# Plain attention: queries and keys projected with heads in partitions, moved to the pairs' rows by DMA; the maxima of four heads turned together

## The reference

```python
x = L0_attn_x                                  # (8, 512, 256) float32
xn = layernorm(x)
x = x + attn_rotary(xn, ...) + ffn(xn, ...)    # both read xn
# ffn(src): 16 heads of 16, this is the part at hand
q = src @ Wq + bq; k = src @ Wk + bk; v = src @ Wv + bv
scores = einsum('bqhd,bkhd->bhqk', q, k) * 16 ** -0.5
attn = softmax(scores) @ v @ Wo + bo
x = layer_norm(src + attn, ln1_g, ln1_b)
# then each row goes through one of 4 experts (256 -> 1024 -> 256), and a second layer_norm
```

## Time and profile before

| | |
|---|---|
| median of 3 runs | 2095.5 us (2095.2 to 2095.9) |
| profiled execution | 2098.55 us, its span 2096.8 us |
| TensorE busy | 1861.5 us (89%) |
| VectorE, ScalarE, GpSimd busy | 1308.8, 915.6, 985.6 us |
| score exponentials of the first phase | 256 x 1025 ns, 248.3 us |
| maxima reductions of the first phase | 512 x 682 ns, 323.2 us |
| maxima products of the first phase | 512, 161.3 us |

### The profile page before, as it was taken

How to read it: one execution, slowest core, us unless ns; L and a number is a source line. 1 busy time by engine, 2 the same in 40 slices (tenths; PEclk the granted TensorE clock), 3 DMA queues, 4 the chain that set the end, 5 groups by cost and what they waited for, 6 DMA issues and landing times.

```text
span 2096.8 us, 36970 instructions
## 1 busy us (share of the span) xinstructions
PE 1861.5 (89%) x12145; PEld 1131.9 (54%) x12146; DVE 1308.8 (62%) x2894; ACT 915.6 (44%) x1313; POOL 985.6 (47%) x681
## 2 busy tenths in 40 slices
PE   5999999999998109999479999999999999999998
PEld 3454544544543109999455555646556565554654
DVE  3767677677675416777676565765656666565661
ACT  2657566566566004444225244252432515335152
POOL 2414133242344353544337637385473855738454
PEclk8999999999999659999779999999999999999999
DMA  6300000000002244566400010100101001010000
GB/s 176 131 1 11 10 0 10 10 0 10 0 0 101 91 176 183 213 213 234 114 11 2 11 32 1 42 2 11 32 1 42 2 11 32 1 42 1 15 18 11
DMA packets 56176, 104.86 MB, mean 50 GB/s; under 512 B 7238, under 2 KB 46566, under 8 KB 50156
## 3 DMA queue, kind: packets, MB, share of 16 engines
q1 hardware_dynamic: 52972, 94.71, 13.4%
q0 software_dynamic: 3072, 8.39, 1.2%
HBM read 76.35 MB, written 26.74 MB: 49 GB/s over the span
## 4 chain that ended last, share of the span: by engine, by line
PE 38%; issue 6%; DVE 3%; POOL 2%; ACT 1%; POOLq 0%; DMA 0%; DVEq 0%; ACTq 0%; SPq 0%
PE a_psS L703 10%; PE a_psO L717 10%; PE a_psO L740 6%; PE a_psM L677 5%; PE a_psS L665 4%; PE a_psS L649 2%; PE a_psS L730 1%; POOL a_k_tok L350 1%; ACT a_probs L468 1%; DVE a_junk L534 1%; POOL a_oT L373 1%; POOL a_q_tok L350 1%; DVE a_alibi L611 0%; DVE a_qL L524 0%; DVE a_rden L548 0%
## 5 line engine op out<-in xcount | busy, mean ns | idle before, releaser
L385 POOL TENSOR_TENSOR a_probs<-a_probs 128x1024 f32<-128x1024 f32 x144 | 340.8, 2393 | 315.9 <-PE a_psO L717 315.9
L534 DVE CUSTOM_DVE_ANT_0 a_junk<-a_psM,a_alibi 128x512 bf16<-128x512 f32 x512 | 333.7, 689 | 215.0 <-PE a_psM L677 214.1
L1282 DVE TENSOR_REDUCE f_q_tok<-f_psR 128x1 f32<-128x512 f32 x512 | 323.2, 682 | 136.6 <-PE f_psR L1437 136.0
L468 ACT ACTIVATE a_probs<-a_psS 128x1024 f32<-128x1024 f32 x256 | 248.8, 1024 | 284.0 <-PE a_psS L703 283.9
L1220 ACT ACTIVATE f_probs<-f_psS 128x1024 f32<-128x1024 f32 x256 | 248.3, 1025 | 64.0 <-PE f_psS L1456 63.4
L717 PE MATMUL a_psO<-a_probs,a_v 128*32 128x512 f32 x2048 | 244.0, 597 | 0.0
L1437 PE MATMUL f_psR<-f_kP,f_qM 64*128 64x512 f32 x512 | 161.3, 498 | 25.6 <-DVE f_q_tok L1282 17.9
L677 PE MATMUL a_psM<-a_kH,a_qH 64*128 64x512 f32 x512 | 126.3, 488 | 34.0 <-DVE a_n_tok L534 29.0
L1469 PE MATMUL f_psO<-f_probs,f_v 128*32 128x512 f32 x1024 | 136.4, 604 | 0.7 <-ACT f_probs L1220 0.6
L740 PE MATMUL a_psO<-a_wo,a_oT 128*128 128x256 f32 x512 | 131.2, 404 | 4.4 <-POOL a_oT L373 4.4
L1843 ACT ACTIVATE e_h<-e_psH,w_o 128x256 f32<-128x256 f32 x152 | 63.8, 471 | 148.7 <-PE e_psH L1935 148.7
(11 more groups left out here) (201 smaller groups left out, 3783.3 us busy)
## 6 DMA issues: line engine op xcount, KB each, us to landing
w_w_high<-w_parts SPq DMA_DIRECT2D x19, 1024.0 KB, 5.5
w_w_low<-w_parts SPq DMA_DIRECT2D x19, 1024.0 KB, 7.6
sorted_x<-f_zeros SPq DMA_DIRECT2D x1, 4864.0 KB, 21.2
e_xs<-sorted_x SPq DMA_DIRECT2D x19, 256.0 KB, 2.7
sorted_z<-e_z SPq DMA_DIRECT2D x19, 256.0 KB, 2.2
f_xn<-in_L_attn_x SPq DMA_DIRECT2D x8, 512.0 KB, 3.5
f_w_raw<-in_L_ffn_W SPq DMA_DIRECT2D x4, 1024.0 KB, 9.2
w_parts<-f_w_high SPq DMA_DIRECT2D x4, 1024.0 KB, 3.9
```

The costliest lines, as they stand in the source:

```text
L385: nc.gpsimd.tensor_tensor(slots, slots, probs[:, first - GRP:first - GRP + 2, :], ALU.add).then_inc(added.sem, 1)
L468: nc.scalar.activation(probs[:, slots, :], psS[:, 2 * p:2 * p + 2, :], ACT.Exp).then_inc(exp_done.sem, 1)
L534: nc.vector.tensor_tensor_reduce(out=junk[:, a, :], in0=psM[:, a, :], in1=alibi[:, h, :], scale=1.0, scalar=-3.0e38, op0=ALU.add, op1=ALU.max,
L1282: nc.vector.tensor_reduce(q_tok[:, c, h, NEG:NEG + 1], psR[:, ring_bank("max", u), :], AX.X, ALU.max, negate=True).then_inc(max_done.sem, 1)
```

## The change

Projection: `project` now has the weights as the stationary operand and the rows of x as the moving one, so that a psR bank holds 128 columns of q or k (64 of each half) by 512 rows of x. The four sides of a batch are keys and queries of the pairs 0 to 3, and keys and queries of the pairs 4 to 7. The weights' columns are put in that order by eight scalings ahead of batch 0. ScalarE takes each side twice out of its bank, whole and high, with the bias (`take_sides`), GpSimd subtracts (`low_part`), and twelve DMAs from SBUF to SBUF for each half of the pairs put the rows where the products want them (`move_sides`): kP and qP, one copy for both kinds of product. The maxima go to a small tile n_tok; when a quad's are complete, four small transposes turn them, ScalarE copies them (4 partitions, n_row), and two DMAs write them to the two rows in qP (`move_maxima`). The 24 groups of transposes of keys and queries are gone. A half is moved when the last scores that read the old one are through (r7 and r15; r is 4 quad + j), and the first maxima product that reads it waits for all twelve (in r10 and, for the second half, in r2 of the next batch). AHEAD is 24 products instead of 20. The projections of queries and keys stand in r4 to r7 instead of r6 to r9, and all maxima products are spread evenly, four a period. On SP the write of zeros, the preloads and the first w1 load come behind the moves of batch 0; stores and loads of w1 for experts 0 and 1 behind those of batch 1. On GpSimd the splits have moved too. VectorE's loop over batches is written out.

```diff
-    AHEAD = MQ + 2
+    AHEAD = 2 * (MQ + 4)
...
     EXTRAS = {(0, 1): [("v", 1)], (0, 2): [("out", 0), ("out", 1)], (0, 3): [("out", 2), ("out", 3)],
-              (1, 2): [("proj", 0)], (1, 3): [("proj", 1)], (2, 0): [("proj", 2)], (2, 1): [("proj", 3)],
+              (1, 0): [("proj", 0)], (1, 1): [("proj", 1)], (1, 2): [("proj", 2)], (1, 3): [("proj", 3)],
               (3, 3): [("v", 0)]}
...
+    TURNED = {(0, 2): [("maxima", 1, 0)], (0, 3): [("rows", 0, 0), ("rows", 1, 2)], (1, 2): [("maxima", 2, 0)],
+              (2, 2): [("maxima", 3, 0)], (3, 2): [("maxima", 0, 0)]}
...
-        quad, j = divmod(r, TT)
-        if quad == QUADS - 1:
-            products = [[0, 1], [2, 3, 4], [5, 6, 7], [8, 9]][j]
-        else:
-            products = [m for m in (AHEAD + 2 * r, AHEAD + 2 * r + 1) if m < QUADS * MQ]
-        return [[2 * m + a for m in part for a in range(2)] for part in (products[:1], products[1:])]
+        first = (AHEAD + 4 * r) % (2 * QUADS * MQ)
+        return [first, first + 1], [first + 2, first + 3]
...
+            def move_sides(b, g):
+
+                if not (isinstance(b, int) and b == 0):
+                    sp.wait_ge(score_ps.sem, score_ps.at(b - 1, QP * (2 * g + 2) * TT - 1))
+                    sp.sem_inc(passed, 1)
+                for i, (pair_rows, kinds) in enumerate(((kP, (high, low, high)), (qP, (high, high, low)))):
+                    n = 2 * g + i
+                    sp.wait_ge(low_done.sem, low_done.at(b, n))
+                    sp.sem_inc(passed, 1)
+                    for a in range(2):
+                        for k, part in enumerate(kinds):
+                            first = FB * a + FH * k
+                            sp.dma_start(pair_rows[first:first + FH, HP * g:HP * (g + 1), :].bitcast(F32),
+                                         part[FB * a:FB * (a + 1), n, :].bitcast(F32)).then_inc(moved[g].sem, 16)
+
+            def move_maxima(b, quad):
+
+                sp.wait_ge(n_row_done.sem, n_row_done.at(b, quad))
+                for a in range(2):
+                    row = FB * a + NEG
+                    sp.dma_start(qP[row:row + 1, QP * quad:QP * (quad + 1), :].bitcast(F32),
+                                 n_row[QP * a:QP * (a + 1), quad % 2, :].bitcast(F32)).then_inc(n_moved.sem, 16)
...
+            sp.wait_ge(zeroed, ZEROED)
+            heads = w["Wo"].rearrange("(q i d) n -> i d q n", i=4, d=FH)
+            for i in range(4):
+                sp.dma_start(wo[32 * i:32 * i + FH, :, :], heads[i]).then_inc(wo_in, 16)
+            move_sides(0, 0)
+            load_rows(0)
+            move_maxima(0, 0)
+            move_sides(0, 1)
+            sp.dma_start(sorted_x.rearrange("(n p) d -> p n d", p=P),
+                         zeros[:, :].unsqueeze(1).to_broadcast([P, TILES * TOK // P, D])).then_inc(cleared, 16)
+            for tile, source in preloads:
+                sp.dma_start(tile, source).then_inc(preloaded, 16)
+
+            def batch(b, more, last):
+                move_maxima(b, 1)
+                move_maxima(b, 2)
+                if more:
+                    if not last:
+                        load_rows(b + 1)
+                    move_sides(b + 1, 0)
+                move_maxima(b, 3)
+                if more:
+                    move_maxima(b + 1, 0)
+                    move_sides(b + 1, 1)
+
             load_w1(0)
-            load_rows(0)
-            for e in range(EARLY):
+            batch(0, True, False)
+            for e in range(NE // 2):
                 store_w1(e)
                 load_w1(e + 1)
-            with sp.Fori(1, B - 1) as b:
-                load_rows(b)
-            for e in range(EARLY, NE):
+            with sp.Fori(1, B - 2) as b:
+                batch(b, True, False)
+            batch(B - 2, True, True)
+            batch(B - 1, False, True)
+            for e in range(NE // 2, NE):
                 store_w1(e)
                 if e + 1 < NE:
                     load_w1(e + 1)
...
+            def low_part(b, n, first=False):
+
+                if not first:
+                    pool.wait_ge(moved[n // 2].sem, moved[n // 2].at(b - 1, 1))
+                    pool.sem_inc(passed, 1)
+                pool.wait_ge(high_done.sem, high_done.at(b, n))
+                pool.sem_inc(passed, 1)
+                nc.gpsimd.tensor_tensor(low[:, n, :], whole[:, n % 2, :], high[:, n, :],
+                                        ALU.subtract).then_inc(low_done.sem, 1)
...
                     norm0.raise_variance(pool, b + 1)
                 if before:
                     normalize(b - 1, QUADS - 1)
-                for e in splits[0:1]:
-                    split_w1(e)
                 add_bias_to_rows(b, not before)
                 if more:
                     keep_rows(b + 1)
+                    low_part(b + 1, 0)
                 normalize(b, 0)
-                for e in splits[1:]:
+                if more:
+                    low_part(b + 1, 1)
+                for e in splits[0:1]:
                     split_w1(e)
-                if more:
...
                 normalize(b, 1)
                 if more:
-                    reset_last(b + 1)
-                    low_last(b + 1)
+                    low_part(b + 1, 2)
+                    low_part(b + 1, 3)
                 if before:
                     scale_rows(b - 1)
                 normalize(b, 2)
                 if before:
                     finish_rows(b - 1)
-
-            batch(0, False, True, range(EARLY))
+                for e in splits[1:]:
+                    split_w1(e)
+
+            batch(0, False, True, range(NE // 2))
             with pool.Fori(1, B - 1) as b:
                 batch(b, True, True)
-            batch(B - 1, True, False, range(EARLY, NE))
...
+            for c in range(KC):
+                for i in range(2):
+                    for g in range(2):
+                        columns = raw[:, c, i, 2 * FB * g:2 * FB * (g + 1)].rearrange("p (e a d) -> p a d e", e=HP, a=2)
+                        nc.scalar.mul(wqk[:, c, 2 * g + i, :].rearrange("p (a d e) -> p a d e", a=2, d=FH), columns,
+                                      FH ** -0.5 if i else 1.0).then_inc(scaled, 1)
...
+            def take_sides(b, n, first=False):
+
+                bank = psR[:, ring_bank("proj", n), :]
+                if not first:
+                    act.wait_ge(moved[n // 2].sem, moved[n // 2].at(b - 1, 1))
+                if not first or n > 1:
+                    act.wait_ge(low_done.sem, low_done.at(b, n - 2))
+                act.wait_ge(proj_ps.sem, proj_ps.at(b, n))
+                nc.scalar.activation(whole[:, n % 2, :], bank, ACT.Identity, bias=bqk[:, n:n + 1])
+                nc.scalar.activation(high[:, n, :], bank, ACT.Identity, bias=bqk[:, n:n + 1]).then_inc(high_done.sem, 1)
...
+                if not first:
+                    act.wait_ge(n_moved.sem, n_moved.at(batch, n - 2))
+                act.wait_ge(nT_ps.sem, nT_ps.at(batch, n))
+                nc.scalar.copy(n_row[:, n % 2, :], psS[0:4, bank, :]).then_inc(n_row_done.sem, 1)
...
+                column = 4 * (pair // 2) + 2 * a + pair % 2
...
-                nc.vector.tensor_reduce(q_tok[:, c, h, NEG:NEG + 1], psR[:, ring_bank("max", u), :], AX.X, ALU.max,
+                nc.vector.tensor_reduce(n_tok[:, c, column:column + 1], psR[:, ring_bank("max", u), :], AX.X, ALU.max,
                                         negate=True).then_inc(max_done.sem, 1)
...
-                        last = nc.tensor.matmul(bank, xnT[:, c, n * P:(n + 1) * P], wqk[:, c, :],
+                        last = nc.tensor.matmul(bank, wqk[:, c, n, :], xnT[:, c, :],
                                                 start=(c == 0), stop=(c == KC - 1))
-                last.then_inc(proj_ps.sem, 1)
+                    last.then_inc(proj_ps.sem, 1)
...
+                else:
+                    pe.wait_ge(max_done.sem, max_done.at(batch, 2 * MQ * (n + 1) - 1))
+                    for t in range(TT):
+                        last = nc.tensor.transpose(psS[0:4, bank, t * P:(t + 1) * P], n_tok[:, t, 4 * n:4 * n + 4],
+                                                   idn[:, :])
+                    last.then_inc(nT_ps.sem, 1)
...
-                batch, half = b + belongs("max", u), HALVES[a]
-                if c == 0 and a == 0:
-                    pe.wait_ge(kP_done.sem, kP_done.at(batch, pair))
-                    pe.wait_ge(qM_done.sem, qM_done.at(batch, pair))
+                batch, half = b + belongs("max", u), slice(FB * a, FB * a + NEG)
+                if c == 0 and a == 0 and pair % HP == 0:
+                    pe.wait_ge(moved[pair // HP].sem, moved[pair // HP].at(batch, 1))
                 bank_read(b, "max", u)
-                nc.tensor.matmul(psR[:, ring_bank("max", u), :], qM[half, pair % 2, c * P:(c + 1) * P],
+                nc.tensor.matmul(psR[:, ring_bank("max", u), :], qP[half, pair, c * P:(c + 1) * P],
```

(47 more changed lines are left out.)

274 lines of the change are left out of this document (77 added, 197 removed).

## The result

The changed kernel takes 2156.7 us (2153.3 to 2162.8, four runs) against 2095.4 us for the kernel before, run beside it: a ratio of 1.0298, 95% interval 1.0269 to 1.0327. Its profiled execution took 2159.9 us, span 2158.1. All of it lies in the first phase: the next one begins (first DMA of w_idn) at 767.00 us instead of 706.39, 60.6 us later.

What follows compares the result with a forecast made beforehand. TensorE was taken to bound the kernel before, waits for the moves afterwards. Six batches +52, start +32, batch 1 +15 and last batch +3 gave +102 us on the median 2095.5: 2197 us, range 2047 to 2220.

Steps and rivals of the forecast that it cites:

- the likeliest one: Main forecast for the whole kernel: moves hold up TensorE twice a batch, 2197 us, own range 2165 to 2220, chance 0.55.
- halves once more from 32 partitions to 16: Assumed rate of the moves' DMAs onto 16 partitions: a quarter of 387 GB/s, 97 GB/s.
- M: Time of one move, twelve DMAs for half the pairs: 16.2 us of transfer plus 2.2 fixed, 18.4 us.
- The batch without stands: Steady batch of the first phase without waits for moves: four pieces together 70.0 us, against 80.4 before.
- The clock loss: After each TensorE stand for a move, four busy microseconds at about half clock: 2 us lost, twice a batch.
- the formula: Steady batch time: 48.2 us plus the larger of 9.2 and M plus the larger of 12.6 and M; 85.0.
- Start +32: One-off cost in batch 0, from late first moves and quad 1's maxima queued behind the zero fill: +32 us.
- Batch 1 and the last: One-off costs: batch 1's output waiting behind the W1 queue and split, +15 us; last batch, split 3 about 3 late, +3.
- Rival 1: Moves are hidden at the 32-partition rate or more: M 10.5 us, 2052 us; chance 0.32 together with Rival 3.
- Rival 2: Moves run halfway, at 135 GB/s: M 13.9 us, 2110 us; chance 0.13.
- Rival 3: VectorE becomes the bound even with short moves: 75 us a batch, 2075 us; chance 0.32 together with Rival 1.
- The signs: Expected in the profile: moves at about 100 GB/s, maxima waits of 5 to 9 us, quad 1 scores waiting some 12 us.

Runs made afterwards that it cites:

- e3: Changed kernel with only one DMA of each six in the moves, most pair rows keeping old values, timing only: 2057.9 us, ratio 0.9825.
- e5: Changed kernel with W1's first store and second load ahead of batch 0's second-half moves, last split after the last normalize: 2139.4 us, ratio 1.0212.
- e10: e8 with quad 0's move put ahead of quad 2's maxima rows and the load of x in SP's queue: 2044.5 us, ratio 0.9766.
- e9: Changed kernel with the two loops that order a half's twelve DMAs exchanged, same DMAs: 2152.2 us, ratio 1.0268.
- e1: Changed kernel with twelve DMAs of half the bytes each (256 of 512 tokens), timing only: 2091.5 us, ratio 0.9973.
- e2: Changed kernel with six whole DMAs of a half's twelve, so half the bytes, timing only: 2081.6 us, ratio 0.9936.
- e7: e4 plus e5's edits, with zero fill, preloads and first W1 load behind quad 1's maxima rows: 2074.3 us, ratio 0.9898.
- e8: e7 with VectorE's inversion of a quad's sums behind the round's second pair of maxima instead of ahead: 2063.5 us, ratio 0.9831.
- e4: Changed kernel projecting and moving by quads, each quad once scored, 48 half-size DMAs a batch for 24: 2108.3 us, ratio 1.0049.

## Why the prediction was right in sign and too high in size

**The mechanism held.** Slower was forecast, and the range 2047 to 2220 holds 2156.7; the likeliest one's own range (2165 to 2220) misses it by 8 us. TensorE waits twice a batch for the last of twelve DMAs with everything queued behind, the granted clock falls to 0.50 after the longer of the two waits and at times after the other, batch 0 waits for the rows of quad 1, batch 1's output for a split of W1, as described. e3, e5 and e10 each take their part away again.

**The move was mis-sized: 18.4 us, measured 14.9 by itself and 11.9 to 14.9 behind a load of x.** The step that failed is the rate: that it "halves once more from 32 partitions to 16", 97 GB/s, was my assumption on top of the 387 and 188 of the earlier trace rows, and no run shows it; the trace has 122 to 126 in a move by itself. The twelve DMAs go to six different groups of 16 partitions, and what e9 rules out is only that their order within the twelve is what counts. What sets the 125, and why a move behind a load of x runs faster once that load is in (151 to 162 in batch 3), was not found. That 12 issues take 6.1 us was also too low: 7.8 us, 0.65 each, since a_wo's were cheaper, 4.08/8 = 0.51. It didn't matter, the transfer being the longer. The stands of the four steady batches: 4.7 to 7.7 us at r10 (9.2 predicted) and 1.0 to 2.6 at r2 (5.8), together 8.6 us a batch for 15.0. With M mis-sized by so much the one at r10 should have been shorter still; the move of batch 3 was issued 1.7 us behind the scores of r7 (291.7 and 293.4), since SP issued the maxima of quad 2 and the load of x ahead of it.

**The batch without stands was too short: 70.0 us, measured 73.5 in e3.** e10, with the inversion moved, has batches of 72.5. The price of VectorE in r0 to r14 was taken as a sum (reductions against products) where single waits of 0.55 to 1.4 us, the longest of them behind an inversion, add up all through the batch.

**The clock loss was too small: 2 us a stand.** In batch 3 the clock is at half from 305 to about 312; about 6 us of work go at half, 3 lost, and nothing is lost behind the second stand. The other batches lose more. Over the four steady ones the stretches at half, nine of them, come to 64.6 us, and TensorE works for 49.7 of these (the sum of the nine windows; PE is the second number):

```profile
sum 64.60, PE 49.71 PEld 17.75 DVE 22.78 ACT 22.83 POOL 21.68; mean PE 5.52 PEld 1.97 DVE 2.53 ACT 2.54 POOL 2.41
```

That is 12.4 us of work at half in each batch where the sum had 8, or 6.2 us lost for 4. Not all of it follows a stand for a move: the stretch from 407.6 to 414.4 comes behind a wait of 1.41 us for VectorE. e10 shows it from the other side: no stand for a move, 0.99.

The errors go against each other. With the measured moves (13.5 us in the mean for first halves, 14.9 for second) the formula gives 48.2 + 28.4 + 4 = 80.6 us a batch, the clock adds 2.2, and 84.1 was measured. That 2197 came within some 40 us of 2157 is in part luck: moves too long by 3.5 to 5 us covered a base and a clock loss too small.

**Start +32, measured +16.** M enters it twice, as 14.9 here (first maxima product at 42.9, not 47.2; r2 at 75.2, not 83), and the wait for quad 1's rows was 5.9 us, not 12. The two rows of the stands in batch 0:

```profile
75.15 0.50 PE L1414 MATMUL f_psR<-f_kP,f_qP 48*128 48x512 f32 x2 [2.29 <-DMA f_qP<-f_low]
...
91.51 1.22 PE L1435 MATMUL f_psS<-f_qP,f_kP 64*128 64x512 f32 x4 [5.92 <-DMA f_qP<-f_n_row]
```

**Batch 1 and the last.** The w1 queue: 15 us predicted in batch 1, 13.1 of wait measured. The last output waited 8.8 us for split 3, before 3.8; "about 3 late" was right within 2.

**The rivals.** Rival 1's move of 10.5 us is what e1 and e2 made (9.6 and 9.1 us), and they came out near the kernel before rather than at 2052: their batches take 76.7 and 75.6 us, not 71.3, with the base too short as above and the clock still at 0.95. Rival 2 was nearest: its M of 13.9 was right within 1 us and its sum of 2110 too low by 47, by the batch of 70.0 us and the clock. Rival 3 was not the bound here, though its 75 us a batch is where the kernels without long waits for moves end (72.5 to 74.2).

**The signs.** The waits for moves, for quad 1's maxima and behind the w1 split came where they were described, with the half clock. The sizes were smaller: 5.9 us and not 12 for the maxima, the last of the twelve lands 5 to 8 us behind its issue and not 12, and the rate is 125 GB/s and not 100.

## What to carry to other kernels

A buffer that is refilled for the next round by DMA need not hold up its reader (in e10 no wait for a move is left in the steady batches) if each part is sent when its last reader is done and not when the last reader of all is done; here the same bytes in twice as many DMAs, 31 us of issues a batch, with the queue ordered by when each entry is ready (and W1, zero fill and inversion moved), turned 2157 into 2044 us (the order of quad 0's move alone is 16 to 19 of them). In one in-order DMA queue look at what stands ahead of each entry: three of the costs here (W1 behind the moves, the maxima behind the zero fill, quad 0 behind the maxima of quad 2) were that. If removing a cause leaves a wait of the same length under another name, a second one ended at the same time: change both before you judge either. And compare the granted clock of two profiles before you explain why their batches differ: between e7 and e8 (0.96 and 0.93), and between e9 and the changed kernel (0.93 and 0.90), it is as large as the difference looked for.

## What the hardware showed that was not expected

- An SBUF to SBUF DMA cost SP 0.6 us of issue whether it moved 64 KB or 128 KB (e4 and the changed kernel), so the small ones were limited by that: 94 to 105 GB/s measured in e4, where 64 KB / 0.635 us is 103.
- A stream of twelve 128 KB DMAs, each onto 16 partitions, runs at 122 to 126 GB/s by itself. Right behind a load of x it can be through 3 us sooner (11.9 us in batch 5, from 457.99 to 469.88), with no cause found. In the median, landing takes 4.6 us (keys) to 6.2 (queries) behind the issue; with 64 KB each 2.2 us.
- DMA share was no measure of the work here: e1 and e2 move the same bytes, 27 GB/s in both from 280 to 360 us, at shares of 0.09 and 0.16.
